# Deformable convolution blocks on one core: the range over partitions by PE transposes, a chunk's offsets in one transfer, and an earlier load of the third chunk's

## What is computed

```python
def _deform_conv2d(x, offset, w, b):
    off = offset.reshape(Bn, K * K, 2, Hh, Ww)
    py = base_y.astype(x.dtype) + off[:, :, 0]
    px = base_x.astype(x.dtype) + off[:, :, 1]
    sampled = jax.vmap(_bilinear_sample)(x, py, px)
    return jnp.einsum('bckhw,ock->bohw', sampled, wk) + b[None, :, None, None]

def _block(x, dc_w, dc_b, of_w, of_b, dw, db):
    h = jax.nn.relu(_deconv2d(x, dc_w, dc_b))
    offset = _conv2d(h, of_w, of_b, PAD)
    return jax.nn.relu(_deform_conv2d(h, offset, dw, db))
```

## Time and profile before

| what | us |
|---|---|
| time, median of three runs | 4393.4 |
| lowest and highest | 4388.1, 4399.3 |
| time of the profiled execution | 4396.3 |
| its span | 4394.4 |
| PE busy in it | 3849.4 (88%) |
| DVE, ACT, POOL busy | 2931.0, 2782.9, 1145.0 |
| chain that ended last, by engine | PE 61%, SP's queue 21%, issue 7%, DMA 3%, POOL's queue 3% |
| chain, SP's two lines | L388 10%, L380 10% |

### The profile page before, as it was taken

How to read it: one execution, slowest core, us unless ns; L and a number is a source line. 1 busy time by engine, 2 the same in 40 slices (tenths; PEclk the granted TensorE clock), 3 DMA queues, 4 the chain that set the end, 5 groups by cost and what they waited for, 6 DMA issues and landing times.

```text
span 4394.4 us, 221688 instructions
## 1 busy us (share of the span) xinstructions
PE 3849.4 (88%) x81888; PEld 2958.5 (67%) x81888; DVE 2931.0 (67%) x5838; ACT 2782.9 (63%) x6651; POOL 1145.0 (26%) x655
## 2 busy tenths in 40 slices
PE   4998799599879869968986996998699999699998
PEld 3676577477657657756765774676577777477776
DVE  4785687388568648846865884785577774477775
ACT  2886588288468738837864882885355554255554
POOL 0341243034134314403422440331121110112111
PEclk8999899799979979988997997999799999799999
DMA  3442544344254334424424442543666664566664
GB/s 118 123 128 68 133 125 113 82 121 127 63 134 126 97 92 126 128 69 128 126 79 110 127 118 73 133 126 113 165 150 155 155 148 127 130 149 152 154 154 108
DMA packets 244839, 533.52 MB, mean 121 GB/s; under 512 B 61200, under 2 KB 151824, under 8 KB 227216
## 3 DMA queue, kind: packets, MB, share of 16 engines
q1 hardware_dynamic: 194224, 498.67, 44.3%
q10 hardware_dynamic: 50240, 29.89, 2.3%
HBM read 471.87 MB, written 56.45 MB: 120 GB/s over the span
## 4 chain that ended last, share of the span: by engine, by line
PE 61%; SPq 21%; issue 7%; DMA 3%; POOLq 3%; ACT 2%; DVE 2%; POOL 0%; ACTq 0%; DVEq 0%; PEld 0%; PEldq 0%
PE P L542 22%; PE PS L560 22%; SPq L388 10%; SPq L380 10%; PE P L513 7%; PE PS L573 7%; POOLq L256 2%; ACT H L840 1%; PE PS L513 1%; DMA X<-x_dram 1%; DMA HB<-off_store 1%; PE P L528 1%; DVE FOFF L1024 1%; DMA off_store<-FOFF 0%; DVE ST L1028 0%
## 5 line engine op out<-in xcount | busy, mean ns | idle before, releaser
L909 DVE TENSOR_TENSOR A<-P,YC 121x384 f32<-121x384 f32 (+1 forms) x4608 | 2312.0, 549 | 959.0 <-ACT YC L760 762.2
L542 PE MATMUL P<-HL,SEL 32*121 32x384 f16 (+1 forms) x21504 | 1730.0, 303 | 323.1 <-issue 216.2
L760 ACT ACTIVATE YC<-P 121x384 f32<-121x384 f32 (+1 forms) x4608 | 1732.5, 445 | 109.5 <-PE P L542 70.8
L542 PEld LDWEIGHTS P<-HL,SEL 32*121 32x121 f16 (+1 forms) x21504 | 1124.0, 116 | 697.1 <-issue 351.6
L560 PE MATMUL PS<-A,VT 121*32 121x80 f32 (+1 forms) x40960 | 1336.5, 249 | 64.2 <-DMA VT<-ht_store 31.7
L560 PEld LDWEIGHTS PS<-A,VT 121*32 121x32 f32 (+1 forms) x40960 | 1087.6, 116 | 366.1 <-issue 203.7
L737 ACT ACTIVATE SMP<-PS 128x480 f32<-128x480 f32 (+3 forms) x1152 | 593.0, 515 | 636.5 <-PE PS L560 630.4
L1089 POOL CAST HL<-DIST 128x1152 f16<-128x1152 f32 x320 | 365.9, 1143 | 2217.2 <-DVE DIST L914 2217.2
L1091 POOL TENSOR_TENSOR HL<-DIST,HL 128x1152 f16<-128x1152 f32 x320 | 769.5, 2405 | 131.6 <-issue 75.7
L727 ACT ACTIVATE DIST<-HB,CONST 128x1152 f32<-128x1152 f32 x320 | 400.8, 1253 | 307.9 <-DMA HB<-off_store 192.8
L573 PE MATMUL PS<-SMP,CW 128*64 128x128 f32 x7424 | 475.9, 277 | 5.4 <-ACT SMP L737 5.4
(11 more groups left out here) (56 smaller groups left out, 740.8 us busy)
## 6 DMA issues: line engine op xcount, KB each, us to landing
HB<-off_store SPq DMA_DIRECT2D x2560, 72.0 KB
VT<-ht_store SPq DMA_DIRECT2D x256, 512.0 KB
VT<-ht_store SPq DMA_DIRECT2D x768, 132.0 KB
VT<-ht_store SPq DMA_DIRECT2D x256, 88.0 KB
off_store<-FOFF SPq DMA_DIRECT2D x160, 128.0 KB, 2.6
H<-x_dram SPq DMA_DIRECT2D x5, 2048.0 KB, 14.2
ht_store<-A ACTq DMA_DIRECT2D x32, 256.0 KB, 3.3
ht_store<-VT ACTq DMA_DIRECT2D x32, 256.0 KB, 4.0
```

Source lines behind the costliest of these rows:

```text
L542: mm = nc.tensor.matmul(dst, SEL[q, table, 0:sh.npos], hats, start=part == 0, stop=part == 1)
L760: nc.scalar.activation(YC[0:sh.npos, g % X_SLOTS, 0:sh.size], P[0:sh.npos, g % Y_SLOTS, 0:sh.size], ACT.Copy).then_inc(y_ready, 1)
L909: return nc.vector.tensor_tensor(dst, x, y, ALU.mult)
```

## The change

Three things are changed, and what they need.

- The maximum over partitions no longer runs on POOL. PE transposes the four numbers of each partition into PSUM (4 x 128), DVE reduces that along the free axis and writes the result 128 times beside itself, PE transposes this back (128 x 4), and DVE reads it from there. Both transposes stand at the end of PE's list for the start of the step; DVE's first new instruction stands behind the clamp of chunk 0.
- `off_store` is laid out by half before image, so that a chunk's offsets are one piece, and are loaded by one DMA with a source of 8 x 16 x 1152 and a target of 128 partitions. The store needs one DMA for each quarter of the partitions, four for each item instead of two.
- Chunk 1's offsets are loaded directly behind chunk 0's, and chunk 2's ahead of the barrier, when chunk 0's distance is done. Chunk 3's are asked for between the windows of chunk 0 and those of chunk 1.

```diff
@@ store_offsets, load_offsets @@
-                for top in range(2):
-                    at = (8 * unit + 4 * top) * BAND_SIZE + image * 2 * CH * CPX
-                    dst = bass.AP(off_store.ap().tensor, at, [[CPX, 2 * CH], [BAND_SIZE, 4], [1, CPX]])
-                    sp.dma_start(dst, FOFF[64 * top:64 * (top + 1), n % OFF_SLOTS, :].rearrange(
+                for j in range(STRIPES):
+                    at = (8 * unit + 4 * (j // 2)) * BAND_SIZE + ((j % 2) * IMG + image) * CH * CPX
+                    dst = bass.AP(off_store.ap().tensor, at, [[CPX, CH], [BAND_SIZE, 4], [1, CPX]])
+                    sp.dma_start(dst, FOFF[CH * j:CH * (j + 1), n % OFF_SLOTS, :].rearrange(
...
-                for i in range(IMG):
-                    for axis in range(2):
-                        at = band * BAND_SIZE + (2 * i + half) * CH * CPX + AXIS * axis * CPX
-                        src = bass.AP(off_store.ap().tensor, at, [[0, AXIS], [1, TAPS * CPX]])
-                        q = CH * i + AXIS * axis
-                        sp.dma_start(HB[q:q + AXIS, half, :], src).then_inc(hb_full[half], 16)
+                at = band * BAND_SIZE + half * IMG * CH * CPX
+                src = bass.AP(off_store.ap().tensor, at, [[AXIS * CPX, 2 * IMG], [0, AXIS], [1, TAPS * CPX]])
+                sp.dma_start(HB[:, half, :], src).then_inc(hb_full[half], 16)
@@ SP, body_of @@
                 load_windows(sh, 0, corners(0, 0))
+                next_offsets(3, 1, 1)
                 load_windows(sh, 1, corners(0, 1))
-                next_offsets(2, 1, 0)
-                next_offsets(3, 1, 1)
                 later_loads()
@@ SP, step @@
                         load_offsets(0, 0)
-                load_offsets(0, 1)
+                        load_offsets(0, 1)
+
+                sp.wait_ge(abs_done, 1)
+                load_offsets(1, 0)
@@ PE, step @@
+                wait_alone(pe, flag_step, 4)
+                nc.tensor.transpose(bank(0)[0:4, 0:128], ST[:, 20:24], IDENT[:, :]).then_inc(flag_step, 1)
+
+                wait_alone(pe, flag_step, 7)
+                nc.tensor.transpose(bank(0)[:, 128:132], TMP[0:4, 0, :], IDENT[0:4, 0:4]).then_inc(flag_step, 1)
@@ DVE, step, behind clamp(0) @@
-                counted(nc.vector.tensor_scalar(ST[:, 28:32], ST[:, 24:28], 1.0 / SCALE, None, ALU.mult))
+                counted(nc.vector.tensor_reduce(ST[0:4, 24:25], bank(0)[0:4, 0:128], AX.X, ALU.max))
+                chained()
+                counted(nc.vector.tensor_scalar(TMP[0:4, 0, :], IDENT[0:4, :], 0.0, ST[0:4, 24:25], ALU.mult, ALU.add))
+
+                flag_count[0] += 1
+                chained()
+                counted(nc.vector.tensor_scalar(ST[:, 28:32], bank(0)[:, 128:132], 1.0 / SCALE, None, ALU.mult))
@@ POOL, step @@
-                pool.wait_ge(flag_step, 4)
-                nc.gpsimd.partition_all_reduce(ST[:, 24:28], ST[:, 20:24], 128,
-                                               bass.bass_isa.ReduceOp.max).then_inc(flag_step, 1)
                 hats(0, 0)
```

16 lines of the change are left out of this document (8 added, 8 removed).

## The result

Before and after ran beside each other on one chip. The changed kernel takes 4323.6 us (median of 4 runs, 4315.7 to 4334.2), the kernel before 4393.5 us (4388.1 to 4399.3). The ratio is 0.984, with a 95% interval of 0.982 to 0.987: 1.6% faster, 70 us. The forecast was 4297 us, 96 us less than before, with a range of 4260 to 4328; the measured time lies near its upper end. Two single runs far above the rest, one of e3's twelve (10,879 us) and one of e8's six (4490 us), are left out of every ratio, and their cause is open.

A forecast was written before the change was run, and what follows sets the result against it. It took PE to bound first groups' chunk loops and SP's DMA issuing second groups', with more lost at step starts. First groups 29, second 50, final 17 make 96 us off 4396.3, less 2.9: 4297 us, range 4260 to 4328.

The forecast's parts named there:

- PE's stop at the start of the branch: Layers' steps, behind the barrier: PE's 9.48 us wait for chunk 2's offsets goes, 9.4 us a step in eight.
- The reload costs 7.33 us in four first groups: POOL before the subtraction, first group of each layer: the remaining library reload still costs 7.33 us.
- The rival for it: POOL, first groups: reload is free when its library is resident; 4.4 us saved in each of four, 4279; chance 0.25.
- The new load lands 2.1 us later, and DVE needs 1.1 us more; SP is through 28.1 us behind its first store: Layers' starts: first distance begins at 92.1 instead of 90.04, so four first groups reach the barrier 2.1 us later.
- Second groups' starts, +0.5 us: Start of four second groups: SP ends at 28.1 us against 28.6, 0.5 us gained each (-3 to +3).
- Second groups: 12.5 us, with a new wait of 3.5 us (0 to 5): Second groups' loops: 9.4 + 3.2 + 3.4 - 3.5 us, taken as 12; the wait is for chunk 4's offsets.
- SP's loop cost, 3.4 us in a second group: Second groups' chunk loop: the SP bound goes, 14 pairs x 0.24 = 3.4 us saved.
- Final steps: Two final steps: 6 us saved up to the barrier and 2.5 from the load of X, 17 in all.
- The 2.5 us from X: Final steps, behind the barrier: 2.5 us (0 to 4) of DVE's 9.54 us wait for X is saved.
- Stores: SP's offset stores in the starts: 0.62 us each whatever the size, sixteen take 10.7 us instead of 7.0.
- The rival of late stores: Second unit, four second groups and final two: sixteen stores at 0.90 us take 14.4 us; 4319 us; chance 0.17.

The follow-up runs named there:

- e3: The changed kernel with the loads in their old order, chunk 2's and 3's offsets asked for behind all eight window loads: 4409.8 us, ratio 1.002.
- e8: The changed kernel with the second groups' 2 MB input load cut into fifteen pieces (a second edit changed nothing): 4297.9 us, ratio 0.979.
- e1: The kernel before with only the range over partitions changed to two PE transposes; stores, loads and order stay: 4355.9 us, ratio 0.991.
- e2: The changed kernel with the range over partitions back on POOL: 4366.2 us, ratio 0.993.
- e6: The changed kernel with chunk 1's offsets asked for behind the second unit's stores instead of right behind chunk 0's: 4310.6 us, ratio 0.983.
- e5: The changed kernel with the transfers as before, two stores an image and eight loads for a chunk's offsets: 4304.4 us, ratio 0.981.
- e9: e5 with the second groups' input load in fifteen pieces and DVE's final-step input wait in front of the first addition: 4295.2 us, ratio 0.979.
- e4: The changed kernel with the second groups' 2 MB input load asked for behind the loop's last windows: 4317.3 us, ratio 0.982.

## Why the prediction was right, and where its sum was not

The time fell in the range, 27 us over the forecast, and the main term was right. Part of the agreement is luck. In the first groups' starts two errors cancel in part: 7.33 us were charged for a reload that costs nothing, and what ends the start comes later than forecast (2.1 us longer were forecast, 0.3 shorter measured). What is missing against the forecast is nearly all in the second groups' loops, 4 x (12 - 5.8) = 25 us. Term by term:

- *PE's stop at the start of the branch*, 9.4 us in each of eight steps. Right: first-group loops are 9.0 us shorter, and e3, which undoes the order alone, puts the stop back (10.92 us).
- *The reload costs 7.33 us in four first groups.* Wrong: it costs nothing (0.26 us as elsewhere). The rival for it had said so, and its mechanism is what e1 and e2 show. But its time, 4279, did not follow, since the gain was lost in the next term.
- *The new load lands 2.1 us later, and DVE needs 1.1 us more; SP is through 28.1 us behind its first store.* This step failed, at both ends. The load was sized as if it were alone. Counted from DVE's first row the distance starts at 21.3 on the mean of the layers' steps instead of 17.8: 1.8 us for the stores in front (2.7 were forecast), 1.7 for the load. From the load's issue it takes 9.0 us where the forecast had 6.6; in e6, where chunk 1's load isn't beside it, 7.5, and before 7.4, with 3 us more of issue. DVE then needs 7.87 us in the first step instead of 5.04 + 1.1, with the two steps that POOL stretches by 0.9 and 1.8. But what ends the start is SP, in seven of eight steps. The second unit's sixteen stores take 10.2 to 12.9 us, 11.9 in the mean, instead of 10.7, and the last lands 5.3 us behind its issue instead of the 3.7 that the sum implies; the barrier comes 30.9 us behind DVE's first row instead of 28.8. e1 shows what is lost by it: its starts are 4.7 us shorter than the changed kernel's in each of eight steps, 38 us. It has the range and its longer chain as well, so the transfers and chunk 1's earlier load are the larger part.
- *Second groups' starts, +0.5 us.* Measured 0.4, by luck: the 28.6 us that SP's end was held against belong to the shortest of the four second groups of before (29.4 from DVE's first row, 31.6 in the mean), and SP comes 2.1 us later than forecast.
- *Second groups: 12.5 us, with a new wait of 3.5 us (0 to 5).* This is the step that made the forecast too low. Chunk 4's offsets come late as foreseen, but by 7 us: their issue is delayed by 12.27 us, as estimated, and the landing was put at 5 us, and is 20 - 12.3 = 7.7. And the stop of PE in chunk 1's samples, 2.6 to 3.3 us, with the lower clock behind it, is in no term; by the estimate above the two take as long by themselves, and in two of the four steps the clock stays low and costs more behind them. Together it is 293.1 - 284.1 = 9 us; e8, which spreads the load, gets 6.3 of them back. No run divides them between the offsets and the stop.
- *SP's loop cost, 3.4 us in a second group*: gone, and PE's round is 17.17 to 17.19 us, 17.14 in first groups. But before it was 17.33 in the mean of a second group, and not the 17.36 of one round against PE's 17.12, so that 14 x 0.15 = 2 us were to be had. SP now waits in the loop.
- *Final steps*: 6 us from the start, measured 5.8, but at another end. The sum has SP end it, 33.1 us behind DVE's first row; SP is there at 28.8 and 29.7, and DVE ends it at 33.5. The 2.5 us from X came as 1.1 in the mean, 3.1 us longer in the first final step and 5.2 shorter in the second: X is asked for 13 us behind the barrier, since SP waits for chunk 1's distance ahead of chunk 3's offsets, and it lands in 23.8 us where it took 17.8.
- *Stores*: "0.62 us whatever its size" was wrong. A store of half the size takes 0.45 us in the second unit of the final steps, and 0.56 to 0.71 (medians) in the layers'. The rival of late stores, 0.90 us each, gave 4319 and would have had the better time, but for a sum that isn't this one: the stores themselves are 1.2 us over the forecast, not 3.7, and most of the 27 us lie in the loops.

Of the three parts, the range is worth 40 us in the old kernel and 41 in the new one. The order is worth 45 us beside the old transfers (e1 to e5) and 84 beside the new ones (e3 to after). The transfers, with chunk 1's load right behind chunk 0's, cost 54 us in the old order (e1 to e3) and some 12 to 15, at the edge of the noise, in the new one (e5 to after; in e5 chunk 1's load is moved too). So each part's worth depends on what stands beside it.

## What to carry to other kernels

Ask for data one branch earlier before you make the request cheaper: what PE waited for was a place in SP's queue. A load merged from eight into one frees the queue but here it had half the engines, so give it to a kernel whose queue is full, and check what its first consumer waits for. And cut a large background load into pieces near the size of the loop's own transfers; laid in front or behind, it stopped the loop here either way. When a wait is found, look also at what PE does just before it: here a stop that no chain shows lay on top of it.

## What the runs showed of the hardware

- Two of DVE's small steps (128x2 and 4x128, from SBUF to SBUF) lasted until POOL's operation ended, 1.95 and 1.17 us instead of 0.16 and 0.27; the one between them that reads PSUM took its 0.16. The Trainium skill (page "SBUF — State Buffer", "SBUF: two separate sides") has DVE and GpSimd share a pair of ports under an exclusive lock for some kinds of DVE instructions, the loser blocked for the whole instruction; the trace agrees.
- A library reload on POOL for a library that was used last costs no time that a trace of 320 calls shows. With two libraries in turn it costs 7.5 us each time (e2: 74.8 in ten, 9.3 the longest).
- Issuing the single load of offsets right behind a 2 MB load took 12.27 us instead of 0.66. In e9 eight loads of offsets took 15.08 us instead of 3.84, though they went out 12 us after two loads of 2 MB. ACT's four stores beside SP's loads once took 9.14 us instead of 3.17. The issue itself lasts longer, and all that is queued behind it waits.
- While a 2 MB load is under way (DMA share 0.94 to 1.03) PE stops for 2.4 to 3.3 us in the midst of a group of matmuls, in all four second groups of the changed kernel and, with the load at the end, of e4. The granted clock falls to 0.50 (1.2 GHz) behind it: for 24, 3, 7 and 17 us in the changed kernel. Behind a stop of 2.63 us in one of its first groups it stays at 1.00.
